# Token sorting and the return of expert outputs in two mixture-of-experts stages of one Trainium2 kernel: table layout, instruction order, and waits between groups of gathers

## The reference, cut to what matters

```python
scores = softmax((x @ wt.T + logits_g) / 2)            # 2048 tokens, 8 experts
topk_w, topk_idx = top_k(scores, 2)                    # normalised weights of two experts
gp = _leaky(einsum('th,ehm->etm', x, w_gate))          # leaky slope 0.01
up = einsum('th,ehm->etm', x, w_up)                    # hidden width 128 per expert
y_all = einsum('etm,emh->eth', gp * up, w_down)
y_sel = y_all[topk_idx, arange(T)[:, None], :]
y = (y_sel * topk_w[..., None]).sum(1).reshape(b, s, h)
p = _leaky(x @ sw_gate) * (x @ sw_up) @ sw_down        # shared experts, width 256
return y + p
```

## Time and profile before

| | |
|---|---|
| runs | 2500.45, 2504.83, 2505.5 us, median 2504.83 |
| the profiled execution | 2498.89 us, its span 2497.0 us |
| mean granted TensorE clock | 0.982 of full speed |
| PE busy | 2355.7 us (94%) |
| PEld busy | 1529.9 us (61%) |
| DVE busy | 1332.7 us (53%) |
| ACT busy | 1074.5 us (43%) |
| POOL busy | 1070.5 us (43%) |
| chain that ended last, by engine | PE 6%, DVE 1%, "another core or an unknown queue" 1% |

### The profile page before, as it was taken

One profiled execution on the slowest core, in us unless ns is written; L12 is line 12 of the kernel. 1 busy time (PEld: TensorE's weight loads), 2 busy tenths in 40 slices (PEclk: granted clock), 3 DMA queues, 4 the chain that ended last, 5 costly groups with the idle time before them and its releaser, 6 DMA issues. The chain is left out here.

```text
span 2497.0 us, 38097 instructions
## 1 busy us (share of the span) xinstructions
PE 2355.7 (94%) x13225; PEld 1529.9 (61%) x13225; DVE 1332.7 (53%) x3171; ACT 1074.5 (43%) x2648; POOL 1070.5 (43%) x1119
## 2 busy tenths in 40 slices
PE   6999999899999989899999999999999988989968
PEld 4555655543444347788686878855665666666736
DVE  7575665557776643243433324356565557764455
ACT  4777676444445423311112111156465644542412
POOL 3654565348777814463121312086564522003430
PEclk9999999989999999999999999999999999999988
DMA  5000000000000042620000010043232310015411
GB/s 170 1 1 1 1 1 22 2 17 14 9 14 13 6 134 88 197 101 1 1 1 0 1 45 1 4 152 121 76 122 89 105 38 1 1 44 166 135 51 39
DMA packets 100319, 124.21 MB, mean 50 GB/s; under 512 B 17666, under 2 KB 79180, under 8 KB 99877
## 3 DMA queue, kind: packets, MB, share of 16 engines
q1 hardware_dynamic: 93156, 102.62, 13.1%
q0 software_dynamic: 6976, 19.15, 2.7%
HBM read 100.97 MB, written 16.56 MB: 47 GB/s over the span
## 5 line engine op out<-in xcount | busy, mean ns | idle before, releaser
L1013 POOL TENSOR_TENSOR cb_sc<-cb_toep,cb_mk 128x128 f32<-128x128 f32 (+3 forms) x256 | 216.1, 873 | 187.6 <-ACT cb_pr L1051 177.4
L1013 POOL TENSOR_TENSOR cb_bias<-cb_bias,cb_mk 128x128 f32<-128x128 f32 (+3 forms) x256 | 215.3, 870 | 146.3 <-DMA cb_bias<-in_fside_16xSxS 146.1
L1654 DVE TENSOR_REDUCE gb_bmax<-PS 128x8 f32<-128x512 f32 x256 | 164.4, 684 | 85.1 <-PE PS L1425 84.5
L389 PE MATMUL PS<-ident,cb_pr 128*128 128x128 f32 x1280 | 198.2, 284 | 4.0 <-ACT cb_pr L1051 2.3
L698 DVE CUSTOM_DVE_ANT_0 cb_sc<-PS,cb_sc,cb_sneg 128x128 f32<-128x128 f32 (+3 forms) x256 | 130.0, 547 | 121.9 <-PE PS L379 118.4
L389 PEld LDWEIGHTS PS<-ident,cb_pr 128*128 128x128 f32 x1280 | 135.0, 140 | 96.2 <-issue 82.0
L1813 ACT ACTIVATE gb_pt<-PS 128x512 f32<-128x512 f32 x256 | 139.2, 596 | 106.1 <-PE PS L1432 101.0
L1057 ACT ACTIVATE cb_pt<-PS 128x128 f32<-128x128 f32 (+3 forms) x448 | 163.6, 414 | 37.9 <-PE PS L389 37.5
L698 DVE CUSTOM_DVE_ANT_0 cb_bias<-PS,cb_bias,cb_sneg 128x128 f32<-128x128 f32 (+3 forms) x256 | 129.4, 547 | 90.0 <-PE PS L379 89.0
L2358 PE MATMUL PS<-eb_g,ff_h 128*128 128x256 f32 x768 | 173.6, 379 | 0.0
L1425 PE MATMUL PS<-gb_ks,gb_qs 32*128 32x512 f32 x512 | 165.8, 649 | 6.5 <-DVE gb_bmax L1654 5.5
(11 more groups left out here) (747 smaller groups left out, 4938.6 us busy)
## 6 DMA issues: line engine op xcount, KB each, us to landing
cb_bias<-in_fside_16xSxS SPq DMA_DIRECT2D x64, 256.0 KB, 2.9
cb_bias<-in_fside_16xSxS SPq DMA_DIRECT2D x64, 192.0 KB, 2.5
ff_h<-in_L_ffn_h_w SPq DMA_DIRECT2D x2, 4096.0 KB
cb_bias<-in_fside_16xSxS SPq DMA_DIRECT2D x64, 128.0 KB, 2.2
y_rows<-eb_g SPq DMA_DIRECT2D x19, 256.0 KB
y_rows<-eb_ys SPq DMA_DIRECT2D x19, 256.0 KB
cb_toep<-rel_table SPq DMA_DIRECT2D x8, 512.0 KB, 6.6
x_rows<-X SPq DMA_DIRECT2D x2, 2048.0 KB, 8.4
```

What stands on the lines that cost most here:

```text
L389: ins = pe.transpose(PS[:, bank, j * P:j * P + P], pr[:, v % 2, e, j * P:j * P + P], ident)
L1013: ins = pool.tensor_tensor(biases(v, e), turned(h, n) if L0 else biases(v, e), mk[:, b % 2, packed(t):packed(t) + n], ALU.add)
L1654: dve.tensor_reduce(bmax[:, n % 2, t, g + e, 0:NB], PS[:, bank + e, :].rearrange("p (n k) -> p n k", k=64), AX.X, ALU.max)\
```

## The change

Both stages: `L`, `Hq`, `Hd` and `rep` keep their number of elements (`rep` a quarter of it) but have 4 in place of 16 as their innermost dimension, so that elements which one product reads lie 8 bytes apart and not 32; the instructions that fill them run over inner runs of four. `rows_of_slots` still sums 32 products.

First stage: TensorE's order is `into(2,0)`, `rows_of_slots`, `into(2,1)`, `down(1)`, `down(2)`. The `leaky` of batch 2 goes from GpSimd to VectorE, with one ScalarE copy in front instead of two. VectorE does `experts_of_tiles` ahead of `leaky(2,1)` and `products(2,1)`. GpSimd issues the gathers of batch 1 only when TensorE has turned the first half of batch 0's sum.

Second stage: `ranks` has one holding product instead of three, `rows_of_slots` none instead of four. GpSimd issues each batch's gathers only when the last ones of the batch ahead have landed.

```diff
@@ sizes shared by both stages @@
+QJ = 4
+NQ = 2 * NJ // QJ
@@ first_experts: the tables (NJ = 16, TILES = 39) @@
-        Hq = cut(2, TILES, NJ, dtype=BF16)
-        Hd = cut(2 * 2 * TILES * NJ, dtype=BF16).rearrange("p (h u t j) -> p h u t j", h=2, u=2, j=NJ)
-        L = flat(yg1).bitcast(BF16).rearrange("p (h m j) -> p h m j", h=2, j=NJ)
-        rep = flat(S4[:, :, :]).bitcast(BF16).rearrange("p (m j) -> p m j", j=NJ)
+        Hq = cut(NQ, TILES, QJ, dtype=BF16)
+        Hd = cut(2 * 2 * TILES * NJ, dtype=BF16).rearrange("p (h u t j) -> p h u t j", h=NQ, u=2, j=QJ)
+        L = flat(yg1).bitcast(BF16).rearrange("p (h m j) -> p h m j", h=NQ, j=QJ)
+        rep = flat(S4[:, :, :]).bitcast(BF16)[:, 0:P * QJ].rearrange("p (m j) -> p m j", j=QJ)
@@ first_experts, TensorE: rows_of_slots @@
-                        h, j = divmod(k, NJ)
+                        h, j = divmod(k, QJ)
                         ins = pe.matmul(PS[:, bank, 0:2 * TILES].rearrange("p (u t) -> p u t", u=2), L[:, h, :, j], Hd[:, h, :, :, j],
                                         start=(k == 0), stop=(k == 2 * NJ - 1))
@@ first_experts, TensorE: the order @@
                 into(2, 0)
+                rows_of_slots()
+                into(2, 1)
                 down(1)
-                into(2, 1)
-                rows_of_slots()
                 down(2)
@@ first_experts, VectorE: the tables @@
-                    halves = lambda x: x.rearrange("p (h k) -> p h k", h=2).unsqueeze(2).to_broadcast([P, 2, TILES, NJ])
-                    link(dve.tensor_tensor(Hq, rep[:, 0:TILES, :].unsqueeze(1).to_broadcast([P, 2, TILES, NJ]), halves(hib[:, :]),
+                    quads = lambda x: x.rearrange("p (q j) -> p q j", j=QJ).unsqueeze(2).to_broadcast([P, NQ, TILES, QJ])
+                    link(dve.tensor_tensor(Hq, rep[:, 0:TILES, :].unsqueeze(1).to_broadcast([P, NQ, TILES, QJ]), quads(hib[:, :]),
                                            ALU.is_equal))
-                    dve.tensor_tensor(Hd[:, :, 1], Hq, halves(colb[:, :]), ALU.mult)
+                    dve.tensor_tensor(Hd[:, :, 1], Hq, quads(colb[:, :]), ALU.mult)
                     dve.tensor_scalar(Hd[:, :, 0], Hq, own, None, ALU.mult).then_inc(sm["mo_column"], 1)
 
                 def hot_slots(k):
-                    dve.tensor_tensor(L[:, k], rep, lob[:, k * NJ:k * NJ + NJ].unsqueeze(1).to_broadcast([P, P, NJ]),
-                                      ALU.is_equal).then_inc(sm["mo_hot"], 1)
+                    half, n = slice(k * NQ // 2, (k + 1) * NQ // 2), NQ // 2
+                    dve.tensor_tensor(L[:, half], rep.unsqueeze(1).to_broadcast([P, n, P, QJ]),
+                                      lob[:, k * NJ:k * NJ + NJ].rearrange("p (q j) -> p q j", j=QJ).unsqueeze(2)
+                                      .to_broadcast([P, n, P, QJ]), ALU.is_equal).then_inc(sm["mo_hot"], 1)
@@ first_experts, VectorE: the order @@
                 hot_slots(0)
                 hot_slots(1)
+                leaky(2, 0)
                 products(2, 0)
                 rows_of_slots()
+                experts_of_tiles()
+                leaky(2, 1)
                 products(2, 1)
-                experts_of_tiles()
                 weights_of_tokens()
@@ first_experts, ScalarE: gate_copy @@
-                    if b < B - 1:
+                    if b < 2:
                         act.activation(lk[:, e, :], PS[:, bank, :], ACT.Copy, scale=0.01)
                         ins = act.activation(gs[:, e, :], PS[:, bank, :], ACT.Relu, scale=0.99)
                     else:
                         ins = act.activation(gs[:, e, :], PS[:, bank, :], ACT.Copy)
@@ first_experts, GpSimd @@
                 def return_rows(b):
-                    if b > 1:
+                    if b == 1:
+                        turned_y.wait_filled(pool, (0, 1, 0))
+                    elif b > 1:
                         pool.wait_ge(sm["mo_y"], b - 1 if b == 2 else b)
...
-                pool.tensor_copy(rep, iota.unsqueeze(2).to_broadcast([P, P, NJ])).then_inc(sm["mo_rep"], 1)
+                pool.tensor_copy(rep, iota.unsqueeze(2).to_broadcast([P, P, QJ])).then_inc(sm["mo_rep"], 1)
                 pool.tensor_copy(colb[:, :], column).then_inc(sm["mo_rep"], 1)
                 for b, e in ((0, 0), (0, 1), (1, 0), (1, 1)):
                     leaky(b, e)
-                leaky(2, 0)
-                leaky(2, 1)
                 pool.wait_ge(sm["mo_rows"], 16)
@@ second_experts, TensorE (the tables, hot_tiles, hot_slots, rep and divmod change as above) @@
                 def ranks():
                     bank = routing.put(pe, "ranks")
-                    hold(bank, 3)
+                    hold(bank, 1)
...
                 def rows_of_slots():
                     bank = routing.put(pe, "rows")
-                    hold(bank, 4)
                     pe.wait_ge(sm["mo_column"], 1)
@@ second_experts, GpSimd @@
                 for b in range(B):
+                    if b:
+                        for k in range(2):
+                            pool.wait_ge(return_sem(b - 1, k, NT - 1), yg_landed)
                     return_rows(b)
                 rows_of_mask(0)
                 rows_of_mask(1)
```

More of the change, by code:

```diff
@@ L3163, in second_experts @@
         cut = Cutter(flat(yg[:, :, :]))
-        L, Hq = cut(2, P, NJ, dtype=BF16), cut(2, TILES, NJ, dtype=BF16)
-        Hd = cut(2 * 2 * TILES * NJ, dtype=BF16).rearrange("p (h u t j) -> p h u t j", h=2, u=2, j=NJ)
+        L, Hq = cut(NQ * P * QJ, dtype=BF16).rearrange("p (h m j) -> p h m j", h=NQ, j=QJ), cut(NQ, TILES, QJ, dtype=BF16)
+        Hd = cut(2 * 2 * TILES * NJ, dtype=BF16).rearrange("p (h u t j) -> p h u t j", h=NQ, u=2, j=QJ)
         assert cut.used <= 2 * YG * D
@@ L3178, in second_experts @@
         slots, prod, over, before = cut(NJ, NE), cut(2, NJ, NE), cut(NE, NJ), cut(NE, NE)
-        rep = flat(wb[:, :, :]).bitcast(BF16).rearrange("p (m j) -> p m j", j=NJ)
+        rep = flat(wb[:, :, :]).bitcast(BF16)[:, 0:P * QJ].rearrange("p (m j) -> p m j", j=QJ)
         above, least, eq, rank = (sb(n, [P, NT]) for n in ("above", "least", "eq", "rank"))
```

## The result

The changed kernel takes 2482.62 us (median of 4 runs, 2479.05 to 2484.41), the kernel before 2503.27 us in the same comparison (4 runs, 2500.45 to 2505.5): ratio 0.9908, 95% interval 0.989 to 0.9926, 20.65 us less. The profiled execution of the changed kernel took 2484.41 us with a span of 2482.6.

The account below looks back on a forecast made before the run. TensorE is busy nearly everywhere; the prediction blamed its stalls on signals held during long gather runs. 13 + 5 + 0.5 + 6 = 24.5 us off the 2504.83 median gave 2480, range 2468 to 2495.

Parts of the forecast that it names:

- The gathers, second stage: Second stage's return: waits between batches of eight gathers let TensorE's held signals through; 13 us off, bounds 3 and 18.5.
- the 18.5 us: Second stage's return: upper bound, no signal held, combine(1, (2, 3)) runs at 2381.8 instead of 2400.27.
- The gathers, first stage: First stage's return: batch 1 waits for batch 0's first turned half, so first_hidden starts earlier; 5 us off.
- The upper bound of 7.4 us: First stage's return: most the delayed batch 1 gathers could gain; the lower bound was 4 us.
- The sort, first stage: First sort: earlier row products, shorter products, against a 2.8 us gap and lower clock; 0.5 us gained, bounds 3 lost, 2.4 gained.
- The sort, second stage: Second sort: less filler and faster row products let gathered rows be turned 4.0 to 8.4 us earlier; 6 us taken.
- the two cases that I gave: Second sort: down(1) takes 3.6 us at full clock or 6.5 us at low clock.
- Tables: Both sorts: VectorE's tables keep their time despite inner runs of four; no change, 2.3 and about 1.4 us at risk.
- Clock: Both sorts: without filler TensorE falls to 1.2 GHz, costing 3 and 2.2 us; 2486, inside the forecast's chance.
- Half cure: Second stage's return: 1.75 us pauses too short after run upon run, gain 3 instead of 13; 2490, chance 0.2.
- full cure: Both returns: no signal held in a run of eight; 32 us off in all, 2472, chance 0.12.
- slower: Both returns: signals held while any gather is under way, waits stretch it by 4 and 8 us; 2510, chance 0.07.

Follow-up runs that it names:

- e6: Kernel before with only the waits between the second stage's gather batches added: ratio 0.9944 to the kernel before.
- e1: Changed kernel with all 32 second-stage gathers issued without waits between batches: ratio 0.996 to the kernel before.
- e2: Changed kernel without the first stage's wait, batches 0 and 1 gathered in one run of 16: ratio 0.9897 to the kernel before.
- e4: Changed kernel with the first stage's order as before on all engines: ratio 0.991 to the kernel before.
- e3: Changed kernel with the tables' inner dimension back at 16: ratio 0.993 to the kernel before.
- e5: Changed kernel with the holding products of the second stage's sort back: ratio 0.9896 to the kernel before.
- e7: Changed kernel without second-stage waits, but a 128x512 GpSimd fill behind each gather there: ratio 0.9941 to the kernel before.
- e12: Changed kernel again, no edit, on the fourth chip: 2463.66 us against 2471.39 for the kernel before, ratio 0.9975.
- e10: Changed kernel with one second-stage wait only, between batches 1 and 2 (two runs of 16), third chip: ratio 0.9979 to the kernel before.
- e9: Changed kernel with 32 extra one-column products before the second stage's router weights of batch 0, third chip: ratio 1.0011 to the kernel before.
- e11: Changed kernel with GpSimd fills behind later batches' gathers instead of waits, both stages, third chip: ratio 1.0031 to the kernel before.
- e8: Changed kernel without second-stage waits, each gathered row cut to 64 columns (output not the reference's): ratio 0.9927 to the kernel before.

## Why the prediction was right, and where it was off

2482.6 us lies in the range and 2.6 us from the forecast of 2480. The measured saving is 20.65 us where the sum had 24.5.

- *The gathers, second stage: 13 us forecast, 11.7 between the profiles, 11 to 15 by e6 and e1.* The cause was right, and it is shown: adding the waits alone removes the lateness, removing them brings it back. What I said about how the rest would go was wrong. Not one signal was held in the second and third run, where I had up to 4 us near each end; `combine(1, (2, 3))` runs 24.8 us behind the first gather (2380.20) and not 42.2, so 17.4 of the 18.5 us came. It was given back by a term that I had as nothing: batch 3 was to be "in time", but VectorE waits for its landing (2397.80). The pause was mis-sized too: a landing 1.75 us after the issue ends is followed by 0.75 us until GpSimd goes on, 2.5 us in all. The forecast's size is partly luck.
- *The gathers, first stage: 5 forecast, 2.7 between the profiles, 0 to 3 by e2.* The first hand-over was freed as forecast (0.5 us instead of 5.8). The upper bound of 7.4 us stands in the prediction without its working; up to the end of the 40 products 7.8 us were indeed won. Behind it I let batch 1's run hold signals by up to 4 us and forgot batch 2's, which starts 1.3 us later: 16 gathers in 21 us over dense products, up to 6.4 us, and 5.1 of the 7.8 us were given back. Of the four terms this is the one whose mechanism failed.
- *The sort, first stage: 0.5 forecast, 1.4 measured (3.1 where the clock stays up).* The gap of 2.8 us in front of `down(2)` is there (2.77). The products came out shorter than I had them (79 ns, not 90 to 100), and e4 and e3 say that all of the gain is the layout's. The lead of the row numbers is hidden, as said. The new order by itself did not pay: at the same clock it is 1.6 us longer than the old one (e4).
- *The sort, second stage: 6 forecast, 6.8 measured*, of which 3.6 are the filler's (e5) and 2.7 the layout's (e3). `down(1)` at 5.38 us lies between the two cases that I gave.
- *Tables: nothing, and nothing measured.*
- *Clock.* I had the fall of the clock as the price of taking filler out. The table in Why this matters for your kernels (the Trainium skill, TensorE: Matmul & The Clock Gate) advises against idle gaps, but against longer ones than the change leaves here: TensorE stands still for 0.87 us before the row products and 1.21 us behind them. So it does not speak against taking this filler out, though the prediction read it so. e5 took 5.16 us with the filler, the changed kernel 5.38 and e1 3.69 without. In the first stage the 16 products took 5.38 us in some executions and 3.69 in others of the same order.
- *The step of 8 bytes.* By the note on cachelines (the Trainium skill, SBUF — State Buffer, Door 1: The DMA port swizzle) it is free. The loads take 117 ns; the nearest packed one took 96. Most of the cost of 147 is gone, and whether the last 21 ns belong to the step was not tried.
- *Half cure, full cure, slower*: none came out. The worst rival, signals held under any gather, is excluded by 2376.23 and by e7.

A thing of another order was not in the prediction at all: on two of the experiments' four chips no signals are held. On one of them the same change is worth 0.25%, 7.7 us (e12). On the other it was not run as it is; taking e10's 2465.24 us and the 4.1 us by which e12's return is longer than e10's, I estimate 2469 us, as much as the kernel before. That kernel is 30 to 38 us quicker on these two chips. No trace of it was kept there, but the stretches allow an estimate: without held signals the two returns take about 41 and 118 us (e10) and not 50.6 and 138.9, which makes 30 us. So held signals in the two returns would explain most of the difference between the chips, and the change wins back about 14 of these 30 us (2.7 and 11.7). The forecast of 2480 was for a chip like the one of the rows.

Open: why signals are held on some chips and not on others, and whether it is the chip at all; whether the amount of TensorE's instructions counts; and whether pace cures the first stage where they are held. e9 to e11 were meant for the last two, and ran where nothing is held. A kernel with runs of 16 or with less pauses was not tried on a chip that holds signals, so no one version is shown to be best on both kinds.

## What to carry to other kernels

When an engine waits ten microseconds for work that is done, look at what GpSimd issues meanwhile, and break the run or slow it; a wait costs about 2.5 us of GpSimd's time each, so first ask who needs the last transfer, and what GpSimd has to do behind it. Filler that is meant to keep the clock up should be checked against the products behind it: here it cost 3.6 us and bought 0.2 at most. Repeat a measurement on another chip before a small gain is credited to its mechanism.

## What the runs showed of the hardware

- With 128-row gathers issued every 1.25 to 1.28 us, TensorE's semaphore signals reached other engines up to 17 us late on the chips of the first comparison, e1 to e8; with one every 1.9 us on such a chip, under 0.1 us (e7). A quarter of the bytes did not cure it: signals up to 15.5 us late, and one that VectorE gives itself 6.5 us late (e8). On the chips of e9 to e12 signals took 0.04 us in runs of 16 too.
- The same kernel took 2501 to 2508 us on some chips (mean granted clock 0.979 to 0.984) and 2469 to 2471 on others (0.986 to 0.989).
- A bf16 matrix product of 78 columns took 79 ns when the elements of both its operands lie 8 bytes apart, 154 when they lie 32 bytes apart, both at full clock, and its weight load 117 and 147. Which operand counts was not tried. 1-column products took 0.16 us for each of 64 passes, with a weight load each (9.95 / 64), at a clock that fell on the way (0.72 over 2357 to 2367).
- TensorE's granted clock fell to half at 954 in the kernel before, while the 32 row products ran without a pause. In e5 the 16 products behind the row products ran at 0.71 in spite of 3.6 us of filler ahead; in e1 the same 16 ran at 1.00 without it.
- A wait of GpSimd on a landing costs 0.7 to 0.8 us beyond the landing.
